# Two planes in turn for the last 40 experts of a mixture-of-experts sum, the third plane loaded early

## The chip, the core and the metric

The kernel runs on one core of a Trainium2 chip. The metric is the device time in microseconds of one execution, as the median of several runs.

## What is computed

Tokens `x` (4 x 1024 rows of 256 floats) go through a cross attention over 77 context rows and the tokens themselves, and then through a mixture of experts: each token picks 8 of 64 experts, every expert computes `silu(x Wg) * (x Wu)` times `Wd` for up to 256 tokens, and the results are weighted and added to the token's row. The part that matters here is the last:

```python
x = x + attention(...)
buf = zeros((E, CAP + 1, h)).at[e, pos_c].set(layernorm(x)[token])[:, :CAP]   # 64 experts, 256 slots each
g = einsum('ech,ehi->eci', buf, w_gate)
u = einsum('ech,ehi->eci', buf, w_up)
y = einsum('eci,eih->ech', silu(g) * u, w_down)
out = zeros((n, h)).at[token].add(y_slots * w_slot[:, None])
x = x + out
```

## The kernel before

The first 880 us are the attention and the routing, which scatters normalised rows, with token number and weights, into a table `slot_rows` in device memory: 256 slots for each of 64 experts. The change doesn't touch them.

The expert loop follows. For each expert e:
- SyncE (SP) loads its 256 slot rows into a ring of 8 buffers (`load_rows`, L975, 321 KB). From expert 8 on it waits until expert e-8 is weighed (`y_made`, L985). Behind the rows of experts 8 to 32, in the same loop, it loads the weights of experts 39 to 63 (L989, 384 KB); the first 39 experts' weights were loaded before.
- TensorE transposes the rows (L1305), multiplies with gate and up weights (L1321) and with the down weights (L1330); ScalarE copies and takes the silu (L1502, L1508), VectorE multiplies (`hidden`, L1743).
- VectorE weighs the result into one of 8 output buffers and takes the token numbers out (`weigh`, L1752, L1753). Expert e needs the buffer of e-8, so it waits until the addition of e-8 has landed (L1750).
- GpSimd (POOL) adds the 256 weighted rows to their tokens' rows in device memory: two indirect DMAs that accumulate, 128 rows of 1 KB each (L1111). Both wait for `y_made` and (L1110) for the plane.

A plane is a copy of the whole output in device memory (4096 rows and some dump rows). There are three: `out` (plane 0), which already holds the attention's result, and `sums` (planes 1 and 2), filled with zeros early on; the profile calls them `out_rows` and `sum`. Expert e is added to plane e % 3. Two experts often have the same token, and additions to one row must not overlap in time, so an expert waits until the one before it on its plane (e-3) has landed in full.

After the loop come the join and the store. SyncE waits for the last addition on plane 1 and loads it in four pieces of 1 MB (128 partitions x 8 KB), then the same for plane 2, then for plane 0 (L996). VectorE adds plane 2 to plane 1 (L1763) and the sum to plane 0 (L1766), piece by piece, and SyncE stores each piece (L1000). Every plane's pieces lie in on-chip memory that held weights or attention data before (`sum_at`, L801 on). Each engine runs its own instructions in the order in which they are written, and so does each queue of DMA issues.

Of the kernel before, what the change touches and what calls it, by code (L numbers as in the profile page):

```python
# [13 lines left out]
ALU = mybir.AluOpType  # L14
# [3 lines left out]
P = 128  # L18
# [13 lines left out]
E, TOPK, G, TG, CAP = 64, 8, 8, 4, 256  # L32
# [3 lines left out]
NTOK = B * S  # L36
# [7 lines left out]
RING = 8  # L44

PLANES = 3
JOIN_PARTS = 4


W_FREE = (16, 22, 39)  # L50
# [565 lines left out]
def build(nc, a, out):  # L616
    with ExitStack() as ctx:
        def sem(name):
            return ctx.enter_context(nc.semaphore(name))

        slot_rows = nc.dram_tensor("slot_rows", [E * CAP, ROW], F32).ap()

        sums = [nc.dram_tensor(f"sum{n}", [NTOK + DUMP, D], F32).ap() for n in range(1, PLANES)]
        names = ["x_loaded", "ctx_loaded", "wqkv_in", "wkvx_in", "qk_g_in", "misc_in", "mask_loaded", "mask_made", "ctx_masked",
                 "const_made", "empty_made", "pads_made", "filled", "vec_step", "pool_step", "stats_done", "z_made", "unit_full",
                 "emptied_act", "emptied_vec", "squares_summed", "rs_made", "normed", "hi_made", "lo_made", "ql_made",
                 "kb_copied0", "kb_copied1", "neg_made", "scores_full", "probs_made", "values_done",
                 "o_copied", "o_scaled", "xres_loaded", "xres_based", "x2_stored", "hn_scaled", "hn_made", "sel_made",
                 "slots_made", "rows_made", "scattered0", "scattered1",

                 *[f"w_early{n}" for n in range(3)], *[f"w_loaded{n}" for n in range(W_BUFS)],
                 *[f"x_in{n}" for n in range(RING)], "rows_turned", "turned_copied", "gate_up", "silu_made", "h_made",
                 "y_full", "y_made", *[f"added{n}" for n in range(PLANES)], *[f"sums{n}_in" for n in range(JOIN_PARTS)],
                 *[f"out{n}_in" for n in range(JOIN_PARTS)], "summed", "stored_out"]
        program(nc, a, out, slot_rows, sums, {n: sem(n) for n in names}, ctx)


# [50 lines left out]
def program(nc, a, out, slot_rows, sums, s, ctx):  # L688
    def sb(name, shape, dt=F32):
        return ctx.enter_context(nc.sbuf_tensor(name, shape, dt))  # L690
# [95 lines left out]
    def parts(t, count, size):  # L786
        return [t[:, size * n:size * (n + 1)] for n in range(count)]
# [11 lines left out]

    size = NTOK // P // JOIN_PARTS * D  # L800
    sum_at = [parts(K1_2, 2, size) + parts(Q0_2, 1, size) + parts(Q1a_2, 1, size),  # L801
              parts(pool_2, 3, size) + parts(Kb_2, 1, size), parts(K0_2, 2, size) + parts(Kb_2, 2, size)[1:]
              + parts(Q1b_2, 1, size)]
    row_ids = sb("row_ids", [P, RING, 2], U32)
    ps_x, ps_g, ps_y = (k.rearrange("p b (t q) -> p b t q", t=2) for k in (ps_s[:, 0:2], ps_u[:, 0:2], ps_o[:, 0:2]))
    slots_dram = slot_rows.rearrange("(e p t) r -> e p t r", p=P, t=2)
# [17 lines left out]
    for e in ("act", "dve"):  # L824
        n = 0
# [47 lines left out]
    def keys_of(pair):  # L873
        return slice(2 * PR, of_tiles(pair).stop)
# [10 lines left out]
    with ExitStack() as inner, nc.Block() as block:  # L885
# [3 lines left out]
        def _(sp):  # L889
# [84 lines left out]
            def load_rows(e):  # L974
                sp.dma_start(xr[e % RING], slots_dram[e]).then_inc(s[f"x_in{e % RING}"], 16)  # L975
# [4 lines left out]
            sp.wait_ge(s["x2_stored"], 16 * 2 * B)  # L980
            for e in range(RING):
                load_rows(e)
            for e in range(RING, E):

                sp.wait_ge(s["y_made"], e - RING + 1)  # L985
                load_rows(e)
                later = e - RING + W_BUFS
                if later < E:
                    sp.dma_start(w_at[later % W_BUFS], a["wexp"][later]).then_inc(s[f"w_loaded{later % W_BUFS}"], 16)  # L989

            plane_v = [k[0:NTOK, :].rearrange("(n p t) d -> n p (t d)", p=P, t=NTOK // P // JOIN_PARTS)
                       for k in (out, *sums)]
            for plane in (*range(1, PLANES), 0):
                sp.wait_ge(s[f"added{plane}"], 32 * len(range(plane, E, PLANES)))
                for n in range(JOIN_PARTS):
                    sp.dma_start(sum_at[plane][n], plane_v[plane][n]).then_inc(  # L996
                        s[f"sums{n}_in" if plane else f"out{n}_in"], 16)
            for n in range(JOIN_PARTS):
                sp.wait_ge(s["summed"], n + 1)
# [4 lines left out]
        def _(pool):  # L1004
# [44 lines left out]
            for t in plan.order["pool"]:  # L1049
# [14 lines left out]
                elif kind == "norm_q":  # L1064
                    b, pair = t[1:]
                    at = KEY_PAIRS * b + pair
                    mine = raw[:, at % 2, 0].rearrange("p a h d -> p a (h d)")
# [4 lines left out]
                elif kind == "lo":  # L1072
                    b, pair = t[1:]
                    at = KEY_PAIRS * b + pair
                    mine = keys_of(pair)
# [4 lines left out]
                elif kind == "ql":  # L1080
# [8 lines left out]
                    for i in range(2):  # L1089
                        mine = slice(PR * i, PR * (i + 1))  # L1090
# [14 lines left out]

            for e in range(E):
                pool.wait_ge(s["y_made"], e + 1)
                if e >= PLANES:
                    pool.wait_ge(s[f"added{e % PLANES}"], 32 * (e // PLANES))
                for t in range(2):  # L1110
                    pool.indirect_dma_start(  # L1111
                        out=(out, *sums)[e % PLANES],
                        out_offset=bass.IndirectOffsetOnAxis(ap=row_ids[:, e % RING, t:t + 1], axis=0),
                        in_=y_out[e % RING][:, t, :], in_offset=None, bounds_check=NTOK + DUMP - 1, oob_is_err=True,
                        compute_op=ALU.add).then_inc(s[f"added{e % PLANES}"], 16)

        @block.tensor
        def _(pe):
# [400 lines left out]
        def _(v):  # L1519
            n_vec = 0  # L1520

            def link(ins):
                nonlocal n_vec
                n_vec += 1
                ins.then_inc(s["vec_step"], 1)
                v.wait_ge(s["vec_step"], n_vec)
# [17 lines left out]
            for t in plan.order["dve"]:  # L1544
# [19 lines left out]
                elif kind == "rs":  # L1564
                    b, pair, piece = t[1:]
# [48 lines left out]
                elif kind == "scale":  # L1614
                    b, x, pr, half = t[1:]
                    mine = slice(2 * P * half, 2 * P * (half + 1))
# [18 lines left out]
                elif kind == "hn_scale":  # L1635
                    b, x, piece, q0, q1 = t[1:]
                    mine = slice(q0, q1)
# [107 lines left out]
            def weigh(e):  # L1745
                r = e % RING
                v.wait_ge(s["y_full"], e + 1)
                if e >= RING:

                    v.wait_ge(s[f"added{(e - RING) % PLANES}"], 32 * ((e - RING) // PLANES + 1))  # L1750
                for t in range(2):
                    v.tensor_scalar(y_out[r][:, t, :], ps_y[:, e % 2, t, :], xr[r][:, t, D + 1 + e:D + 2 + e], None, ALU.mult)  # L1752
                v.tensor_copy(row_ids[:, r, :].unsqueeze(2), xr[r][:, :, D:D + 1]).then_inc(s["y_made"], 1)  # L1753

            hidden(0)
            for e in range(1, E):
                hidden(e)
                weigh(e - 1)
            weigh(E - 1)
            for n in range(JOIN_PARTS):  # L1760
                v.wait_ge(s[f"sums{n}_in"], 16 * (PLANES - 1))
                for plane in range(2, PLANES):
                    link(v.tensor_tensor(sum_at[1][n], sum_at[1][n], sum_at[plane][n], ALU.add))  # L1763
            for n in range(JOIN_PARTS):
                v.wait_ge(s[f"out{n}_in"], 16)
                v.tensor_tensor(sum_at[0][n], sum_at[0][n], sum_at[1][n], ALU.add).then_inc(s["summed"], 1)  # L1766
# [44 lines left out]
```

## Time and profile before

| | us |
|---|---|
| median of 3 runs | 1169.75 (1168.24 to 1171.47) |
| span of the profiled execution (first to last instruction) | 1168.4 |
| TensorE busy | 906.8 (78%) |
| VectorE busy | 655.7 (56%) |
| GpSimd busy | 581.3 (50%) |
| ScalarE busy | 463.0 (40%) |
| expert loop, from GpSimd's first addition to its last issue | 889.1 to 1127.5 |
| join and store | 1127.5 to 1168.4 |

Busy shares of the span are averages over stages with different limits, so they don't tell what bounds the last 280 us. The rows below are of that stretch. Times in them are microseconds from the start of the span, unless a column says ns.

### The profile page before, as it was taken

The page shows a single profiled execution, that of the slowest core. Times are in us where ns is not written, and L with a number is a line of the kernel's source. Part 1 is how long each engine was busy: PE and PEld are TensorE (multiplying, and loading weights), DVE is VectorE, ACT ScalarE, POOL GpSimd, SP SyncE. Part 2 cuts the span into 40 slices and gives each one's busy share as a digit, 9 for nine tenths or more (in the row PEclk, how much of TensorE's full clock was granted, in tenths as well). Part 3 has the DMA queues.
Part 4 walks back from the last instruction along what each step waited for, and adds up shares of the span by engine and source line. Part 5 has one row for each costly group of instructions (what it writes and reads, how often), then busy time and mean ns, then how long its engine had stood idle before and what let it go on. Part 6 is the DMA issues. An engine that isn't in the chain of part 4 may idle for free.

```text
span 1168.4 us, 13234 instructions
## 1 busy us (share of the span) xinstructions
PE 906.8 (78%) x3848; PEld 626.7 (54%) x3848; DVE 655.7 (56%) x1956; ACT 463.0 (40%) x930; POOL 581.3 (50%) x522
## 2 busy tenths in 40 slices
PE   3869999999999999999964973957308999889300
PEld 2545666556656656656532542846207888777200
DVE  4475647875789775888652743743533443333206
ACT  3734675545755646664430521333103333222000
POOL 3530231204755635655665073155554888888850
PEclk9879999999999999999986995968658999999755
DMA  7739602012221422101261102000428999999689
GB/s 249 267 111 386 218 3 72 20 31 90 77 78 58 132 84 87 55 23 67 78 239 54 37 29 87 24 24 9 171 88 244 308 312 188 158 159 152 70 231 392
DMA packets 85335, 150.77 MB, mean 129 GB/s; under 512 B 14090, under 2 KB 53050, under 8 KB 83216
## 3 DMA queue, kind: packets, MB, share of 16 engines
q1 hardware_dynamic: 54543, 112.32, 27.8%
q0 software_dynamic: 30720, 37.61, 16.3%
q8 instruction: 32, 0.52, 0.2%
q14 instruction: 40, 0.32, 0.1%
HBM read 69.19 MB, written 97.45 MB: 143 GB/s over the span
## 4 chain that ended last, share of the span: by engine, by line
PE 48%; DVE 13%; issue 11%; POOL 8%; another core or an unknown queue 7%; DMA 7%; ACT 4%; POOLq 0%; SPq 0%; ACTq 0%; DVEq 0%
PE ps_o L1257 15%; PE ps_u L1154 6%; POOL sum L1111 4%; PE ps_s L1233 4%; PE ps_s L1235 4%; PE ps_u L1177 4%; DMA out_rows<-again,row_ids 3%; PE ps_u L1269 2%; PE ps_o L1252 2%; POOL out_rows L1111 2%; PE ps_u L1321 2%; DVE mp L1580 2%; PE ps_u L1165 2%; DMA sum<-again,row_ids 2%
## 5 line engine op out<-in xcount | busy, mean ns | idle before, releaser
L1044 POOL DMA_INDIRECT slot_rows<-rows,slot_idx x256 | 251.2, 981 | 312.0 <-issue 137.5
L1580 DVE TENSOR_REDUCE mp<-ps_u 128x1 f32<-128x512 f32 x256 | 165.1, 686 | 103.2 <-remote 49.6
L1450 ACT ACTIVATE probs<-ps_s 128x512 f32<-128x512 f32 x256 | 139.9, 596 | 176.6 <-PE ps_s L1235 105.4
L1111 POOL DMA_INDIRECT sum<-again,row_ids x84 | 130.0, 1548 | 26.5 <-issue 22.6
L1257 PE MATMUL ps_o<-probs,pool 128*128 128x512 f32 (+1 forms) x288 | 138.0, 602 | 2.5 <-ACT den L1471 2.5
L1321 PE MATMUL ps_u<-again 128*128 128x256 f32 x512 | 123.9, 386 | 0.0
L1257 PE MATMUL ps_o<-probs,V 128*128 128x512 f32 (+1 forms) x216 | 106.4, 615 | 10.4 <-ACT probs L1453 5.9
L1235 PE MATMUL ps_s<-qbT,Kb 65*128 65x512 f32 (+1 forms) x252 | 102.4, 406 | 0.0
L1752 DVE TENSOR_SCALAR again<-ps_o,again 128x256 f32<-128x256 f32 x128 | 56.1, 480 | 82.3 <-DMA sum<-again,row_ids 54.7
L1154 PE MATMUL ps_u<-wqkv_s,lnT 128*128 128x512 f32 (+1 forms) x256 | 97.4, 515 | 4.1 <-ACT lnT L1373 3.2
L1321 PEld LDWEIGHTS ps_u<-again 128*128 128x128 f32 x512 | 94.2, 194 | 11.0 <-issue 0.3
L1059 POOL TENSOR_TENSOR pool<-pool,rs_y 128x1024 f32<-128x1024 f32 (+1 forms) x20 | 33.0, 1649 | 131.9 <-DVEq L1575 130.8
L1111 POOL DMA_INDIRECT out_rows<-again,row_ids x44 | 68.3, 1551 | 27.4 <-DVE row_ids L1753 14.5
L1330 PE MATMUL ps_o<-again 128*128 128x256 f32 x256 | 67.1, 384 | 14.5 <-DVE again L1743 14.2
L1257 PEld LDWEIGHTS ps_o<-probs,pool 128*128 128x128 f32 (+1 forms) x288 | 53.4, 192 | 44.0 <-issue 28.1
L1502 ACT ACTIVATE again<-ps_s 128x512 f32<-128x512 f32 x64 | 38.2, 597 | 95.5 <-PE ps_s L1305 86.3
L1177 PE MATMUL ps_u<-K,Q 128*128 128x512 f32 x128 | 56.9, 518 | 22.6 <-DVE mp L1580 21.5
L1233 PE MATMUL ps_s<-Q,K 128*128 128x512 f32 x144 | 68.6, 476 | 4.5 <-issue 2.4
L1154 PEld LDWEIGHTS ps_u<-wqkv_s,lnT 128*128 128x128 f32 x256 | 48.9, 199 | 40.4 <-issue 27.8
L1743 DVE TENSOR_TENSOR again<-again,ps_u 128x256 f32<-128x256 f32 x64 | 26.8, 418 | 70.4 <-ACT again L1508 64.0
L1257 PEld LDWEIGHTS ps_o<-probs,V 128*128 128x128 f32 (+1 forms) x216 | 40.4, 195 | 43.0 <-issue 20.5
L1330 PEld LDWEIGHTS ps_o<-again 128*128 128x128 f32 x256 | 47.7, 190 | 25.7 <-DVE again L1743 19.7
(190 smaller groups left out, 1610.8 us busy)
## 6 DMA issues: line engine op xcount, KB each, us to landing
again<-in_wexp SPq DMA_DIRECT2D x64, 384.0 KB, 5.3
slot_rows<-rows SPq DMA_DIRECT2D x2, 10272.0 KB, 35.0
again<-slot_rows SPq DMA_DIRECT2D x64, 321.0 KB
sum<-rows SPq DMA_DIRECT2D x2, 4352.0 KB, 27.6
again<-sum SPq DMA_DIRECT2D x8, 1024.0 KB, 11.3
Kb<-K SPq DMA_DIRECT2D x16, 275.5 KB
pool<-in_x SPq DMA_DIRECT2D x4, 1024.0 KB, 5.5
xres<-in_x SPq DMA_DIRECT2D x8, 512.0 KB
```

The source lines that it names most:

```text
L1044: pool.indirect_dma_start(out=slot_rows, out_offset=bass.IndirectOffsetOnAxis(ap=slot_idx[x][:, q, k:k + 1], axis=0), in_=rows[x][:, q, :] ...
L1111: pool.indirect_dma_start(out=(out, *sums)[e % PLANES], out_offset=bass.IndirectOffsetOnAxis(ap=row_ids[:, e % RING, t:t + 1], axis=0), in ...
L1154: i = pe.matmul(dst, lnT[0:w, at % 2, c, 0:rj], rhs, start=(c == 0), stop=(c == 1))
L1177: pe.matmul(bank((*t, i))[:, :], queries(b, x)[0][:, 2 * pr + i, tile * P:(tile + 1) * P], K[b % 2][:, 2 * pr + i, half * 512:(half + 1) * ...
L1233: pe.matmul(dst, K[b % 2][:, h, kt * P:kt * P + rk], queries(b, x)[0][:, h, :], start=True, stop=False)
L1235: pe.matmul(dst, Kb[:, h, kt * P:kt * P + rk], qbT[block_no[(b, x, pr)] % 2][:, hh, :], start=False, stop=True).then_inc(s["scores_full"], 1)
L1257: i = pe.matmul(ps_o[:, hh, :], V[b % 2][0:rk, pr, kt, DH * hh:DH * hh + P], probs[0:rk, n % NPR, hh, :], start=(kt == 0), stop=(kt == NKT ...
L1321: i = pe.matmul(ps_g[:, e % 2, which, :], w_at[e % W_BUFS][:, o:o + I], xT[e % 2][:, k, :], start=(k == 0), stop=(k == 1))
L1330: i = pe.matmul(ps_y[:, e % 2, t, :], hid[e % 2][:, t * P:(t + 1) * P], w_at[e % W_BUFS][:, 4 * I:4 * I + D], start=True, stop=True)
L1450: act.activation(probs[:, n % NPR, hh, :], ps_s[:, u % NSC, :], ACT.Exp).then_inc(s["probs_made"], 1)
L1580: v.tensor_reduce(mp[:, i, tile, half:half + 1], bank((*t, i))[:, :], AX.X, ALU.max).then_inc(s["emptied_vec"], 1)
L1752: v.tensor_scalar(y_out[r][:, t, :], ps_y[:, e % 2, t, :], xr[r][:, t, D + 1 + e:D + 2 + e], None, ALU.mult)
```

## The change

Experts 0 to 23 are added to planes 0, 1, 2 in turn as before. Experts 24 to 63 are added to planes 1 and 0 in turn (24 to 1, 25 to 0, ... 62 to 1, 63 to 0). So every wait for a plane from expert 26 on is for the landing of e-2 instead of e-3, and plane 2 is complete when expert 23 has landed. Plane 2 is loaded in 16 pieces of 256 KB (128 partitions x 2 KB), one behind each of the row loads of experts 46 to 61, so when experts 38 to 53 have been weighed; ahead of the first stands a wait for plane 2's last addition. After the loop SyncE loads only plane 1 and plane 0. Some pieces of the planes get other places on chip. VectorE does the same eight additions as before.

```diff
+EARLY = 24
+EARLY_PIECES = 4
+EARLY_FROM = 46
+
+
+def plane_of(e):
+    return e % PLANES if e < EARLY else (e + 1) % (PLANES - 1)
+
+
+def plane_count(plane, end):
+    return sum(plane_of(e) == plane for e in range(end))
...
     sum_at = [parts(K1_2, 2, size) + parts(Q0_2, 1, size) + parts(Q1a_2, 1, size),
-              parts(pool_2, 3, size) + parts(Kb_2, 1, size), parts(K0_2, 2, size) + parts(Kb_2, 2, size)[1:]
-              + parts(Q1b_2, 1, size)]
+              parts(pool_2, 3, size) + parts(K0_2, 1, size),
+              parts(Kb_2, 2, size) + parts(probs_2, 1, size) + parts(Q1b_2, 1, size)]
...
                     sp.dma_start(w_at[later % W_BUFS], a["wexp"][later]).then_inc(s[f"w_loaded{later % W_BUFS}"], 16)
 
-            for plane in (*range(1, PLANES), 0):
-                sp.wait_ge(s[f"added{plane}"], 32 * len(range(plane, E, PLANES)))
+                piece = e - EARLY_FROM
+                if piece == 0:
+                    sp.wait_ge(s["added2"], 32 * plane_count(2, E))
+                if 0 <= piece < JOIN_PARTS * EARLY_PIECES:
+                    n = piece // EARLY_PIECES
+                    width = size // EARLY_PIECES
+                    mine = slice(width * (piece % EARLY_PIECES), width * (piece % EARLY_PIECES + 1))
+                    sp.dma_start(sum_at[2][n][:, mine], plane_v[2][n][:, mine]).then_inc(s[f"early{n}_in"], 16)
+
+            for plane in (1, 0):
+                sp.wait_ge(s[f"added{plane}"], 32 * plane_count(plane, E))
                 for n in range(JOIN_PARTS):
                     sp.dma_start(sum_at[plane][n], plane_v[plane][n]).then_inc(
                         s[f"sums{n}_in" if plane else f"out{n}_in"], 16)
...
                 pool.wait_ge(s["y_made"], e + 1)
-                if e >= PLANES:
-                    pool.wait_ge(s[f"added{e % PLANES}"], 32 * (e // PLANES))
+                plane = plane_of(e)
+                if plane_count(plane, e):
+                    pool.wait_ge(s[f"added{plane}"], 32 * plane_count(plane, e))
...
-                    v.wait_ge(s[f"added{(e - RING) % PLANES}"], 32 * ((e - RING) // PLANES + 1))
+                    plane = plane_of(e - RING)
+                    v.wait_ge(s[f"added{plane}"], 32 * plane_count(plane, e - RING + 1))
...
             for n in range(JOIN_PARTS):
-                v.wait_ge(s[f"sums{n}_in"], 16 * (PLANES - 1))
-                for plane in range(2, PLANES):
-                    link(v.tensor_tensor(sum_at[1][n], sum_at[1][n], sum_at[plane][n], ALU.add))
+                v.wait_ge(s[f"early{n}_in"], 16 * EARLY_PIECES)
+                v.wait_ge(s[f"sums{n}_in"], 16)
+                link(v.tensor_tensor(sum_at[1][n], sum_at[1][n], sum_at[2][n], ALU.add))
```

## Rows read from the trace of the kernel before

**Rows 1.** Timeline, GpSimd (start, duration, what, idle before): first addition, last five.

```profile
889.10 1.58 POOL L1111 DMA_INDIRECT out_rows<-again,row_ids  x1 [13.90 <-DVE row_ids L1753]
...
1118.51 1.54 POOL L1111 DMA_INDIRECT sum<-again,row_ids  x1 [0.30 <-issue]
1120.36 1.55 POOL L1111 DMA_INDIRECT sum<-again,row_ids  x1 [0.30 <-issue]
1122.22 1.54 POOL L1111 DMA_INDIRECT sum<-again,row_ids  x1 [0.30 <-issue]
1124.07 1.55 POOL L1111 DMA_INDIRECT out_rows<-again,row_ids  x1 [0.30 <-issue]
1125.92 1.54 POOL L1111 DMA_INDIRECT out_rows<-again,row_ids  x1 [0.30 <-issue]
```

**Rows 2.** The page's costliest groups: busy us, mean ns of one, idle before.

```profile
L1111 POOL DMA_INDIRECT sum<-again,row_ids x84 | 130.0, 1548 | 26.5 <-issue 22.6
```

**Rows 3.** Waits from 880 to 1130 us: us in total, times, longest.

```profile
DVE again L1752 <- DMA sum<-again,row_ids: 54.7, 24, 5.3
...
POOL sum L1111 <- DMA sum<-again,row_ids: 1.5, 2, 0.9
POOL sum L1111 <- DMA out_rows<-again,row_ids: 1.2, 4, 0.3
```

**Rows 4.** Windows: length, busy PE, PEld, DVE, ACT, POOL; clock, DMA share, GB/s.

```profile
926.00:963.00 37.00, 37.00 (x197) 32.56 (x197) 17.24 (x49) 11.97 (x25) 29.82 (x21) 1.00 1.10 308
1002.00:1064.00 62.00, 52.12 (x258) 43.58 (x258) 21.85 (x69) 15.70 (x32) 51.94 (x34) 0.97 0.92 159
...
1138.00:1158.00 20.00, 0.00 (x0) 0.00 (x0) 16.01 (x7) 0.00 (x0) 0.00 (x0) 0.50 1.01 427
```

**Rows 5.** Timeline, VectorE: weighing that starts as experts 22, 28, 32, 42, 48, 55 land.

```profile
980.41 0.88 DVE L1752 TENSOR_SCALAR again<-ps_o,again 128x256 f32<-128x256 f32 x2 [2.27 <-DMA sum<-again,row_ids]
...
1002.99 0.88 DVE L1752 TENSOR_SCALAR again<-ps_o,again 128x256 f32<-128x256 f32 x2 [5.33 <-DMA sum<-again,row_ids]
...
1016.85 0.88 DVE L1752 TENSOR_SCALAR again<-ps_o,again 128x256 f32<-128x256 f32 x2 [4.41 <-DMA sum<-again,row_ids]
...
1054.78 0.88 DVE L1752 TENSOR_SCALAR again<-ps_o,again 128x256 f32<-128x256 f32 x2 [5.33 <-DMA out_rows<-again,row_ids]
...
1075.56 0.88 DVE L1752 TENSOR_SCALAR again<-ps_o,again 128x256 f32<-128x256 f32 x2 [3.81 <-DMA out_rows<-again,row_ids]
...
1100.10 0.88 DVE L1752 TENSOR_SCALAR again<-ps_o,again 128x256 f32<-128x256 f32 x2 [2.78 <-DMA sum<-again,row_ids]
```

**Rows 6.** Timeline, GpSimd: the second addition of expert 22.

```profile
973.89 1.56 POOL L1111 DMA_INDIRECT sum<-again,row_ids  x1 [0.30 <-issue]
```

**Rows 7.** Chain that ended last (start, us, what): two landings, weights being loaded.

```profile
928.34 7.12 DMA sum<-again,row_ids
...
939.47 7.15 DMA sum<-again,row_ids
```

**Rows 8.** From a release to GpSimd's start: chain at expert 18, timeline before expert 0.

```profile
955.78 0.04 issue
955.82 0.03 POOLq L1111
...
956.58 1.55 POOL out_rows L1111
...
888.09 0.16 DVE L1753 CAST row_ids<-again 128x2 uint32<-128x2 f32 x1
```

**Rows 9.** One line, L975: the row loads' issues (ns min/median/max, first, last start).

```profile
L975 SPq DMA_DIRECT2D again<-slot_rows x64: 319/320/710, 876.4 to 1071.5; - x64
```

**Rows 10.** The join: timeline of SyncE and VectorE, and two pieces of the chain.

```profile
1122.32 11.73 SPq L996 DMA_DIRECT2D again<-sum  x8
1138.60 1.76 SPq L996 DMA_DIRECT2D again<-out_rows  x4
...
1125.92 12.66 DMA out_rows<-again,row_ids
...
1139.93 18.27 DMA again<-out_rows
...
1158.22 2.29 DVE L1766 TENSOR_TENSOR again<-again 128x2048 f32<-128x2048 f32 x1 [0.18 <-DMA again<-out_rows]
```

More of the change, by code:

```diff
@@ L633, in build @@
                  "y_full", "y_made", *[f"added{n}" for n in range(PLANES)], *[f"sums{n}_in" for n in range(JOIN_PARTS)],
-                 *[f"out{n}_in" for n in range(JOIN_PARTS)], "summed", "stored_out"]
+                 *[f"early{n}_in" for n in range(JOIN_PARTS)], *[f"out{n}_in" for n in range(JOIN_PARTS)], "summed", "stored_out"]
         program(nc, a, out, slot_rows, sums, {n: sem(n) for n in names}, ctx)
@@ L982, in _ @@
                 load_rows(e)
+            plane_v = [k[0:NTOK, :].rearrange("(n p t) d -> n p (t d)", p=P, t=NTOK // P // JOIN_PARTS)
+                       for k in (out, *sums)]
             for e in range(RING, E):
@@ L989, in _ @@
                     sp.dma_start(w_at[later % W_BUFS], a["wexp"][later]).then_inc(s[f"w_loaded{later % W_BUFS}"], 16)
-            plane_v = [k[0:NTOK, :].rearrange("(n p t) d -> n p (t d)", p=P, t=NTOK // P // JOIN_PARTS)
-                       for k in (out, *sums)]
-            for plane in (*range(1, PLANES), 0):
-                sp.wait_ge(s[f"added{plane}"], 32 * len(range(plane, E, PLANES)))
+                piece = e - EARLY_FROM
[8 more added lines that the diff above has]
+                sp.wait_ge(s[f"added{plane}"], 32 * plane_count(plane, E))
                 for n in range(JOIN_PARTS):
@@ L1107, in _ @@
                 pool.wait_ge(s["y_made"], e + 1)
-                if e >= PLANES:
-                    pool.wait_ge(s[f"added{e % PLANES}"], 32 * (e // PLANES))
+                plane = plane_of(e)
+                if plane_count(plane, e):
+                    pool.wait_ge(s[f"added{plane}"], 32 * plane_count(plane, e))
                 for t in range(2):
                     pool.indirect_dma_start(
-                        out=(out, *sums)[e % PLANES],
+                        out=(out, *sums)[plane],
                         out_offset=bass.IndirectOffsetOnAxis(ap=row_ids[:, e % RING, t:t + 1], axis=0),
                         in_=y_out[e % RING][:, t, :], in_offset=None, bounds_check=NTOK + DUMP - 1, oob_is_err=True,
-                        compute_op=ALU.add).then_inc(s[f"added{e % PLANES}"], 16)
+                        compute_op=ALU.add).then_inc(s[f"added{plane}"], 16)
         @block.tensor
```

## The prediction

> **What bounds the kernel now.** I read the profile from its end backwards, because the change touches the last 280 us only. The first view is the timeline of GpSimd (POOL). It issues two accumulating DMAs for each of the 64 experts, from 889.10 to 1125.92 us [rows 1]. A DMA costs 1.55 us of GpSimd time [rows 2] and 0.30 us pass before the next, so an expert costs 3.71 us (1120.36 to 1124.07) [rows 1]. 64 experts at 3.71 us are 237 us, and the stretch from 889.10 to 1127.47 is 238.4 us: GpSimd issues back to back for the whole loop. The list of waits says the same from the other side. VectorE waits 54.7 us for additions to land, because its ring of eight outputs is full, while GpSimd's waits for a landing are of 0.3 to 0.9 us each [rows 3]. TensorE, ScalarE, VectorE and the loads are ahead of GpSimd, and only GpSimd's issue, then the join of the planes after 1127.47 us, sets the end. The chain that ended last names VectorE and DMAs in places in this stretch; these are coincidences in time, since GpSimd had no idle time there.
>
> The join is bound by the DMA engines: from 1138 to 1158 us their share is 1.01 at 427 GB/s [rows 4]. One plane is 4.19 MB, thus 4.19 / 0.427 = 9.8 us.
>
> **What a landing takes, and who waits for it.** This decides the case. An expert may be added to a plane only when the previous expert on that plane has landed. I call L the time from the end of an expert's second issue to its landing. The profile gives no landing directly for every expert, but VectorE starts to weigh expert e+8 0.1 us after e has landed, so its rows give L [rows 5]. The ends of the issues follow from one row, 973.89 + 1.56 = 975.45 us for expert 22 [rows 6], and 3.707 us for each expert after it.
> - Quiet, after the last row load (expert 55): landing at 1100.0, issue ended at 1097.8, L = 2.2 us.
> - With the slots' rows being loaded (321 KB for each expert), L alternates. The short ones are 2.2 to 3.2 us. The long ones, on even experts from 22 to 48, are 4.9, 3.9, 4.2, 5.2, 3.2, 4.2, 4.7, 3.8, 4.2, 4.2, 5.1, 3.6, 3.1 and 3.6 us; the rows of 22, 28, 32, 42 and 48 stand in the group [rows 5].
> - With weights loaded too (705 KB for each expert, 308 GB/s in all instead of 159 [rows 4]), the chain shows 7.12 and 7.15 us from the start of a second issue, so L = 5.6 us [rows 7].
>
> How late may a landing be? After a landing GpSimd needs time to start. At 955.82 us its sequencer takes up expert 18, whose plane had just been freed, and the DMA starts at 956.58; with the 0.04 us ahead of that it is 0.80 us [rows 8]. The very first DMA agrees: VectorE's row ends at 888.25, the DMA starts at 889.10, 0.85 us [rows 1, 8]. I take 0.84. With three planes the wait is for expert e-3, two whole experts (7.41 + 0.30 us) lie between, and L may be 6.9 us. The case of expert 18 is the only one in which a landing exceeded that, and so the wait is as good as free now. With two planes only one expert lies between: 3.71 + 0.30 - 0.84 = 3.16 us. **Every landing over 3.16 us stalls GpSimd by the difference**, and GpSimd is the bound.
>
> **Part 1, two planes from expert 24 on.** The wait at line 1110 becomes one for e-2. Behind it on GpSimd's queue stands only the next expert, but VectorE, SyncE's row loads and TensorE hang on the same landings, and all of them have slack. Putting the 14 long landings as they were against 3.16 us gives 1.7 + 0.7 + 1.0 + 2.0 + 0 + 1.0 + 1.6 + 0.6 + 1.0 + 1.1 + 1.9 + 0.4 + 0 + 0.4 = 13.4 us. The odd experts use the other plane, and their landings stay under 3.2 us, so they add nothing. After expert 48 L is 2.2 us, and nothing stalls. Of these, experts 22 to 28 have 5.4 us and 30 to 46 have 7.6 us. Does a stall heal itself by letting the loads pass first? Partly it may. But a landing also releases the row load (SyncE's issue follows it through VectorE), and in the stalled order expert e+2's second DMA goes out 0.84 + 3.40 = 4.2 us after e's landing, when these loads are on their way. So I do not count on it.
>
> **Part 2, sixteen loads of 256 KB during experts 38 to 53.** Line 985 lets them go when those experts are weighed, so at the landings of experts 30 to 45, at about 1008 to 1064 us. Their issue costs SyncE about 0.3 us each, as the row loads do [rows 9], which is hidden since SyncE waits for VectorE most of that time. The second issue of expert 23 ends at 979.2 us (one step behind that of 22 [rows 6]); with any landing seen here it is down by 987, and the first piece comes after 1008 us, so the added wait for plane 2 does not hold the row loads queued behind it. What they cost is landing time. Bytes per expert rise from 321 to 577 KB; the nearest rows on either side are the long landings here (4.0 us on average for 30 to 46) and those under weights at 705 KB (5.6 us). At the unchanged pace the line between them gives 4.0 + 256/384 x 1.6 = 5.1 us; a stalled loop, with about 4.5 us to an expert, moves 577/4.5 = 128 GB/s of loads against 321/3.71 = 87 before and 705/3.71 = 190 under weights, and by that measure it is 4.0 + 41/103 x 1.6 = 4.6 us. I take 4.6, since the pace will be the stalled one. Two experts then share one stall of 4.6 - 3.16 = 1.44 us: 8.5 x 1.44 = 12.2 us for experts 30 to 46 instead of 7.6. Bounds: the loads add nothing and part of the 13.4 us heals, which I put at 8 us, or L reaches the 5.6 us seen with weights (8.5 x 2.44 = 20.7, in all 26.5 us).
>
> Loop, taken value: 5.4 + 12.2 + 0.4 = **18.0 us longer**, between 8 and 26.5.
>
> **Part 3, the join.** Now: loads of plane 1 issued at 1122.32, when expert 61 has landed, 5.15 us ahead of GpSimd's end T = 1127.47; the last addition starts at 1158.22 = T + 30.75; the span ends at 1168.4, 10.2 us later [rows 10]. After: 4.19 MB less, 9.8 us off. Against it plane 1 now ends with expert 62, so its loads begin one expert later relative to T, 3.7 us. In its favour the stream meets fewer additions: today those of experts 62 and 63 land inside it (the last one 12.66 us after its issue began [rows 10]), four DMAs; afterwards at most those of 63. Each reads 128 KB here and 128 KB of the plane; 0.26 MB at 427 GB/s are 0.6 us, so about 2 us for three of them. Sum: 9.8 - 3.7 + 2.1 = **8.2 us shorter**. Bounds are 6 (no relief, a short gap before the loads of the last plane) and 9.8. VectorE has the same eight additions, all but the last behind loads. New places of the buffers and the extra semaphores cost nothing on a path.
>
> Sum: 1168.4 + 18.0 - 8.2 = 1178.2 us of span. The median of the runs stands 1.35 us above this span, so **1179.5 us** is forecast.
>
> A rule of the Trainium skill is weighed here, in sentences that nothing else needs. In the trace a quiet landing takes L = 2.2 us [rows 5, 6]. The page "DMA: Bandwidth & Descriptors", section "Anatomy of one DMA", gives a GpSimd DMA a fixed 2.0 us plus its bytes over 436 GB/s, so an estimate of 2.3 us for 128 KB, and calls the fixed part about constant. By that rule alone no landing would reach 3.16 us and part 1 would be free; the quiet rows agree, the rows under load (3.2 to 5.6 us) don't, and the measurement decides. The same page says (section "SWDGE vs HWDGE vs iDMA") that an engine serves its queues in turn, which speaks against the change: every load's packets would stand between an addition's. In the join, with megabytes of loads on the way, the last addition lands 12.66 - 1.55 = 11.1 us after its issue [rows 10], which agrees.
>
> **The rivals.**
> - *Faster: landings stay short.* The stalls shift the additions so far that the loads pass between them and L stays at the quiet 2.2 us or little above. For it: every second landing in the stretch already is under 3.2 us. Against it: 12 of the 14 others are over, and the new loads hang on the same landings. It decides where all stalls together are under 8.2 us. Only the join's gain is left, 1169.75 - 8.2 = 1161.5 us, up to 1166 with a few stalls.
> - *Even: the loop loses what the join gains.* The stalls are 5 to 12 us: the loads add nothing and part of the 13.4 us heals. That is 1166.5 to 1173.5 us, about 1169.
> - *Slower still: contention as with weights.* L = 5.6 us while the pieces run: 1169.75 + 26.5 - 8.2 = 1188 us. For it: the DMA share already is 0.92 there [rows 4]. Against it: fewer bytes than with weights.
> - *The early load saves nothing in the join* since the last addition's landing, not the loads, sets it. With the last landing at T + 11.1 as now and 4.19 MB behind it the join would still be some 7 us shorter; this changes the sum by 1 to 2 us and lies inside the range.
>
> **How the numbers follow.** My forecast's mechanism with 12 to 23 us of stall (1173.5 to 1184.5): 0.62. Even: 0.16. Faster: 0.10. Slower still, over 23 us: 0.12. The range is 1167 to 1190 us: it leaves out the faster rival and the far ends. A measurement of this kernel can tell 0.3%, 3.5 us, from no change. Faster by more: 0.10; within: 0.16; slower by more: 0.74.
>
> **What would show it.** In the profile after: GpSimd's last issue ends at about 1145 instead of 1127.5, with idle times of 0.5 to 2 us ahead of every second expert from 24 to 48, released by DMAs on out_rows and sum (wrong if they stay at 0.30); none after expert 50. From GpSimd's end to the end of the span 32 to 34 us instead of 40.9. The DMA share from 1010 to 1075 at about 1.0 and over 190 GB/s. The early loads land well before the join. The prediction is wrong if landings under the early loads stay below 3.2 us, or if SyncE or VectorE, not a landing, becomes what GpSimd waits for.

## The result

The changed kernel takes 1181.96 us, the kernel before 1168.99 us (medians of 6 runs each on one chip). The ratio is 1.0107 (95% interval 1.0083 to 1.0131): the change makes the kernel 13 us slower. The profiled execution has a span of 1179.4 us against 1168.4. These 11.0 us split into three parts that the trace gives directly:

| us | before | after | difference |
|---|---|---|---|
| start of the first addition | 889.1 | 891.5 | +2.4 |
| loop, first addition to the end of the last issue | 238.4 | 254.5 | +16.1 |
| join, from there to the end of the span | 40.9 | 33.4 | -7.5 |

The first part lies ahead of everything that was changed. The same start is anywhere from 886.8 to 892.2 in the profiles of five other kernels below with unchanged work ahead of it, so it is not counted as an effect.

### The profile page after: what moved, and what is told of

The parts are those of the page before. It is cut to its first block, busy times and chain, and to the rows that moved or that the text cites. A ratio compares the mean times of both kernels' runs of the same rounds, so it can differ in the third digit from the quotient of the medians.

```text
span 1179.4 us, 13247 instructions
## 1 busy us (share of the span) xinstructions
PE 914.5 (78%) x3848; PEld 631.8 (54%) x3848; DVE 654.0 (55%) x1956; ACT 462.5 (39%) x930; POOL 580.4 (49%) x522
## 4 chain that ended last, share of the span: by engine, by line
PE 52%; DVE 12%; issue 11%; POOL 8%; DMA 6%; another core or an unknown queue 5%; ACT 5%; POOLq 0%; SPq 0%; ACTq 0%; DVEq 0%
PE ps_o L1278 16%; PE ps_u L1175 6%; PE ps_s L1254 4%; PE ps_u L1198 4%; PE ps_s L1256 4%; POOL sum L1132 4%; PE ps_u L1342 3%; POOL out_rows L1132 3%; DMA out_rows<-again,row_ids 3%; PE ps_o L1273 2%; PE ps_u L1290 2%; PE ps_u L1186 2%; DMA sum<-again,row_ids 2%; PE ps_o L1351 2%
## 5 line engine op out<-in xcount | busy, mean ns | idle before, releaser
L1132 POOL DMA_INDIRECT sum<-again,row_ids x72 | 111.4, 1548 | 29.7 <-issue 18.4
L1132 POOL DMA_INDIRECT out_rows<-again,row_ids x56 | 86.7, 1549 | 40.6 <-issue 16.9
L1351 PE MATMUL ps_o<-again 128*128 128x256 f32 x256 | 71.3, 403 | 24.5 <-DVE again L1764 24.4
```

What stands on the lines that cost most here:

```text
L1132: pool.indirect_dma_start(out=(out, *sums)[plane], out_offset=bass.IndirectOffsetOnAxis(ap=row_ids[:, e % RING, t:t + 1], axis=0), in_=y_o ...
L1351: i = pe.matmul(ps_y[:, e % 2, t, :], hid[e % 2][:, t * P:(t + 1) * P], w_at[e % W_BUFS][:, 4 * I:4 * I + D], start=True, stop=True)
```

## The profile after

First GpSimd's timeline around experts 35 to 40 (start, duration, what, idle before and what ended it). Before, every idle time here was 0.30 us. Two rows belong to each expert; 1026.29 is the first of expert 35.

```profile
1026.29 1.55 POOL L1132 DMA_INDIRECT out_rows<-again,row_ids  x1 [1.57 <-DMA out_rows<-again,row_ids]
1028.14 1.55 POOL L1132 DMA_INDIRECT out_rows<-again,row_ids  x1 [0.30 <-issue]
1029.99 1.55 POOL L1132 DMA_INDIRECT sum<-again,row_ids  x1 [0.30 <-issue]
1031.84 1.54 POOL L1132 DMA_INDIRECT sum<-again,row_ids  x1 [0.30 <-issue]
1035.19 1.55 POOL L1132 DMA_INDIRECT out_rows<-again,row_ids  x1 [1.80 <-DMA out_rows<-again,row_ids]
1037.04 1.56 POOL L1132 DMA_INDIRECT out_rows<-again,row_ids  x1 [0.30 <-DVE row_ids L1775]
1038.91 1.56 POOL L1132 DMA_INDIRECT sum<-again,row_ids  x1 [0.31 <-issue]
1043.34 1.54 POOL L1132 DMA_INDIRECT sum<-again,row_ids  x1 [2.87 <-DMA out_rows<-again,row_ids]
1045.19 1.55 POOL L1132 DMA_INDIRECT out_rows<-again,row_ids  x1 [0.30 <-issue]
1047.04 1.54 POOL L1132 DMA_INDIRECT out_rows<-again,row_ids  x1 [0.31 <-issue]
1049.36 1.55 POOL L1132 DMA_INDIRECT sum<-again,row_ids  x1 [0.77 <-DMA sum<-again,row_ids]
```

VectorE's timeline shows two of the landings (it starts 0.1 us after one), those of experts 35 and 37:

```profile
1034.44 0.88 DVE L1774 TENSOR_SCALAR again<-ps_o,again 128x256 f32<-128x256 f32 x2 [5.55 <-DMA out_rows<-again,row_ids]
...
1042.98 0.88 DVE L1774 TENSOR_SCALAR again<-ps_o,again 128x256 f32<-128x256 f32 x2 [5.72 <-DMA out_rows<-again,row_ids]
```

L is again the time from the end of an expert's second issue to its landing. Expert 35's second issue ends at 1029.69 and it lands at 1034.35, so L = 4.7 us. Expert 37, next on its plane, starts 0.84 us later, at 1035.19, and GpSimd has idled 1.80 us instead of 0.30. That is the stall as the prediction has it, 4.7 - 3.16 = 1.5 us. The other kind was not foreseen. At 1043.34 the **second** DMA of expert 38 (on plane 1) starts 2.6 us late, though expert 38 waits for nothing between its two DMAs. It starts 0.46 us after the landing of expert 37 at 1042.88, the one for which the **next** expert, 39, waits.

Adding up these rows over the loop (each idle time less the usual 0.30): 10.2 us at first DMAs, nearly all of it at nine between experts 29 and 52, and 7.5 us at second DMAs: experts 38 (2.6) and 45 (3.1), and 7, 19, 31 and 59 with 0.4 to 0.5 each. Before, the two kinds were 0.4 and 0.9 us.

The list of waits of GpSimd from 963 to 1150 us (us in total, times, longest) tells the same with the usual 0.30 in it, against [rows 3]:

```profile
POOL out_rows L1132 <- issue: 13.2, 33, 3.4
POOL sum L1132 <- issue: 12.3, 40, 0.4
POOL out_rows L1132 <- DMA out_rows<-again,row_ids: 7.3, 5, 1.9
POOL sum L1132 <- DMA sum<-again,row_ids: 6.2, 5, 1.9
POOL sum L1132 <- DMA out_rows<-again,row_ids: 2.9, 1, 2.9
POOL out_rows L1132 <- DMA sum<-again,row_ids: 1.9, 3, 0.8
```

Windows as in [rows 4] (length, busy PE, PEld, DVE, ACT, POOL; clock, DMA share, GB/s). GpSimd is busy 44.43 of 62 us instead of 51.94; more is moved (185 GB/s instead of 159), and yet the DMA share fell from 0.92 to 0.86. Fewer additions in the same time fit this: in no_rows_no_pieces (below), where only additions are under way, they alone take a DMA share of 0.61 for 70 GB/s (920 to 980 us).

```profile
1002.00:1064.00 62.00, 51.16 (x235) 42.26 (x236) 17.69 (x56) 14.14 (x29) 44.43 (x30) 0.92 0.86 185
```

The join, which answers to [rows 10], in the timeline. Plane 1's loads are issued at the landing of expert 62, plane 0's at that of 63, and the last addition of the planes starts at 1169.23, 23.3 us after GpSimd's end at 1145.95 (30.75 before).

```profile
1144.47 2.04 SPq L1016 DMA_DIRECT2D again<-sum  x4
...
1154.55 1.76 SPq L1016 DMA_DIRECT2D again<-out_rows  x4
...
1169.23 2.29 DVE L1788 TENSOR_TENSOR again<-again 128x2048 f32<-128x2048 f32 x1 [0.18 <-DMA again<-out_rows]
```

## The experiments

The time of a run scatters by several us, and one chip ran all kernels some 85 us faster than the others (before: 1086 us on it, about 1170 elsewhere; the clock granted to TensorE was 0.92 there against 0.89). On it ran no_rows_pieces, no_rows_no_pieces, ring2048 and the first switch_51. The loop and the join are read from the trace of each kernel; switch_51, profiled on the fast chip and on a slower one, has 241.5 us of loop on both, so they are compared across chips. The loop is the stretch from the first addition to the end of the last issue, as above. "First" and "second" are the idle times at first and second DMAs, less 0.30 each. Most rows are a single profile.

| | loop | first | second | join |
|---|---|---|---|---|
| before | 238.4 | 0.4 | 0.9 | 40.9 |
| after | 254.5 | 10.2 | 7.5 | 33.4 |
| planes_only | 247.2 | 5.3 | 5.1 | 43.5 |
| loads_only | 237.5 | 0.0 | 0.5 | 40.6 |
| no_rows_pieces | 246.9 | 2.8 | 7.3 | 34.1 |
| no_rows_no_pieces | 240.0 | 0.0 | 3.0 | 42.9 |
| spaced_waits | 257.7 | 12.6 | 8.3 | 33.2 |
| ring2048 | 269.6 | 4.8 | 27.9 | 33.1 |
| ring5120 | 250.9 | 13.6 | 0.6 | 33.6 |
| late_switch | 245.1 | 4.3 | 3.7 | 34.7 |
| switch_51 (two profiles) | 241.5, 241.5 | 2.4, 2.4 | 2.2, 2.1 | 33.4, 33.9 |

**planes_only: two planes, no early load.** Plane 2 is loaded in the join behind plane 1.

```diff
-                piece = e - EARLY_FROM
...
-            for plane in (1, 0):
+            for plane in (1, 2, 0):
```

> The changed kernel, but plane 2 is loaded in the join, behind plane 1, in 4 pieces of 1 MB; no early loads. Theory (a landing over 3.16 us stalls GpSimd by the difference, and the early loads lengthen the landings): the loop is 8 to 13 us longer than before (254.5 us in the changed kernel, 238.4 before), so 3 to 8 us less than in the changed kernel; the join is 3.7 us less the saved additions, so 1 to 3 us longer than the 40.9 us of before. In all 10 to 16 us over before. Rival (the early loads are what costs, the planes are free): the loop stays within 2 us of 238.4 and the time within 1 to 4 us of before. Rival (the early loads cost nothing): the loop is 254 us as in the changed kernel, and the time 17 to 20 us over before.

Loop 247.2, join 43.5 us. Timed, it is 1.0161 of before (1.0118 to 1.0204), 1188.0 against 1172.4 us; the trace explains 8.8 + 2.6 = 11.4 of these 15.6 us, the rest is open. Neither rival holds: the two planes alone cost 8.8 us of the loop, the early loads the other 7.3. And the early load brings 43.5 - 33.4 = 10.1 us in the join, near the 9.8 us reckoned for one plane. So the early load by itself gains 10.1 - 7.3 = 2.8 us; what loses are the two planes that make room for it, 8.8 us in the loop and 2.6 in the join. GpSimd's waits from 963 to 1136 us:

```profile
POOL sum L1123 <- DMA out_rows<-again,row_ids: 3.2, 4, 1.8
POOL sum L1123 <- DMA sum<-again,row_ids: 2.9, 3, 1.4
POOL out_rows L1123 <- DMA sum<-again,row_ids: 2.7, 3, 1.6
POOL out_rows L1123 <- DMA out_rows<-again,row_ids: 2.2, 2, 1.3
```

**loads_only: three planes, with extra loads.** They read the input x, so nothing of the sums is left out.

```diff
-    return e % PLANES if e < EARLY else (e + 1) % (PLANES - 1)
+    return e % PLANES
...
-                    sp.dma_start(sum_at[2][n][:, mine], plane_v[2][n][:, mine]).then_inc(s[f"early{n}_in"], 16)
+                    sp.dma_start(sum_at[2][n][:, mine], x_v[n][:, mine]).then_inc(s[f"early{n}_in"], 16)
```

> Three planes throughout as before, but with 16 extra loads of 256 KB at the places of the early loads; they read the input x instead of a plane (same shape) and are overwritten in the join, where all three planes are loaded as before. Theory: the long landings of experts 30 to 45 rise from 4.0 to 4.3 or more us on average, but with three planes they may take 6.9 us, so GpSimd issues back to back, the loop stays 238 to 239 us and the time is within 0.3% of before. Rival (the loads slow GpSimd's own work or the DMA engines are at their limit): gaps or longer issues on GpSimd, loop over 241 us.

Ratio 0.9985 (0.9955 to 1.0015), loop 237.5. The loads do what they were expected to do to the landings: of each two experts from 30 to 46 the later landing takes 4.6 us on average, 4.1 without the loads, and the mean of all rises from 3.3 to 4.1. With three planes GpSimd doesn't wait for it. Here the loads have no price of their own; they have one through a wait that is short of slack. GpSimd's waits, none over 0.3 us, and the windows row from 1010 to 1070, with a DMA share of 1.04:

```profile
POOL sum L1133 <- DMA out_rows<-again,row_ids: 0.3, 1, 0.3
...
1010.00:1070.00 60.00, 50.90 (x255) 41.36 (x255) 20.97 (x66) 15.70 (x32) 50.25 (x33) 1.00 1.04 224
```

**no_rows_pieces and no_rows_no_pieces: the row loads taken away.** The changed kernel and planes_only, both with

```diff
+                if e < LAST_ROWS:
                     load_rows(e)
```

where `LAST_ROWS` is 40; TensorE's wait for the rows is changed to match.

> The changed kernel without the row loads of experts 40 to 63: these experts work on the rows left in the ring (loads left out, so the output is not the reference's). The early loads stay. So from the landing of expert 24 on only 256 KB follow each landing instead of 577 KB. Theory (the landing is lengthened by what is loaded at the same time): long landings fall to 3 to 4 us, stalls and late second DMAs together to 2 to 7 us instead of 17.7 in the changed kernel, loop 240 to 245 us. Rival (an addition lands late for a reason of its own, the plane's rows or a shorter distance between additions to one plane): landings of 4 us and more and a loop over 250 us.

> As the kernel with two planes and the whole plane 2 loaded in the join (planes_only), but also without the row loads of experts 40 to 63 (they work on the rows left in the ring, so the output is not the reference's). Nothing is loaded between the landing of expert 24 and the join. Theory: every landing from 26 on takes 2.2 to 2.4 us, under 3.16, so there is no stall and no late second DMA on two planes, and the loop is 238 to 240 us as with three planes; the join stays 43 to 44 us. Rival (two planes stall by themselves): stalls at every second expert as in planes_only, loop 245 us or more.

With nothing loaded, every landing from expert 25 to 55 takes 2.1 to 2.4 us (VectorE's rows show no later ones), and no first DMA waits. So the distance of one expert is enough by itself, and the stalls at first DMAs come from what is loaded beside. One expectation failed: second DMAs are late here too, by 0.5 to 0.6 us at experts 31, 38, 45, 52 and 59, always 0.46 us after the landing of the expert before. VectorE's rows show three landings 3.7 us apart, as GpSimd issues, the quiet case:

```profile
908.03 0.88 DVE L1767 TENSOR_SCALAR again<-ps_o,again 128x256 f32<-128x256 f32 x2 [2.08 <-DMA out_rows<-again,row_ids]
...
911.74 0.88 DVE L1767 TENSOR_SCALAR again<-ps_o,again 128x256 f32<-128x256 f32 x2 [2.43 <-DMA sum<-again,row_ids]
...
915.50 0.88 DVE L1767 TENSOR_SCALAR again<-ps_o,again 128x256 f32<-128x256 f32 x2 [2.49 <-DMA out_rows<-again,row_ids]
```

With the early loads only, the first DMAs' stalls are 2.8 us, but both kinds together are 10.1 us against the expected 2 to 7, and the loop is 246.9, over the expected 245, again through the second DMAs of 38 and 45 (2.4 and 2.0 us). Landings of 4.1 and 4.2 us are still seen (experts 33, 37, 40), over the expected 3 to 4. The rival, an addition that is late for a reason of its own, is refused by no_rows_no_pieces, not by this kernel.

**spaced_waits and ring2048: what makes second DMAs late?** The late ones on two planes are at most of 31, 38, 45, 52 and 59, 14 DMAs apart. (Among the first experts, on three planes, they are at some of 7, 13 and 19, 12 apart.) Two edits, one in the instruction stream and one in the size of the memory in which GpSimd writes its descriptors:

```diff
+                for _ in range(2):
+                    pool.wait_ge(s["filled"], 16 * FILLS)
```

```diff
-    nc = bacc.Bacc("TRN2", target_bir_lowering=False, num_devices=1, dynamic_dma_scratch_size=4096)
+    nc = bacc.Bacc("TRN2", target_bir_lowering=False, num_devices=1, dynamic_dma_scratch_size=2048)
```

> The changed kernel with two more instructions on GpSimd behind each expert's second DMA, waits on a semaphore that has long been full. In the changed kernel the second DMAs of experts 38 and 45 start 2.6 and 3.1 us late, both 0.46 us after the landing for which the next expert waits, as if the wait behind the DMA held it. If that is so and depends on where the wait lies in the instruction stream, the late second DMAs vanish or are at other experts than 31, 38, 45 and 59, and the time is up to 6 us less. If they are due to the data or to the loads, they stay at 38 and 45 and the time is that of the changed kernel.

> The changed kernel with half the on-chip memory for the descriptors that GpSimd writes (2048 bytes instead of 4096, the compiler's setting). So far the second DMAs that start late are 14 DMAs apart at most places (experts 31, 38, 45, 52, 59), whatever stands in the instruction stream. If they belong to the wrap of this memory, they come twice as often: every 7 DMAs, so every 3 or 4 experts, at second DMAs and perhaps at first ones, and the loop is 5 to 12 us longer than 254.5. If they don't, they stay at 38 and 45 and the loop at 253 to 258 us.

The additional waits left them where they were (38 by 3.2 us, 45 by 3.4), ratio 1.0118 (1.006 to 1.0175). But they left only one row of their own in the trace in place of 128, so it is open whether they changed what GpSimd executes, and as a test of the instruction stream this is weak. The halved memory is clear: late second DMAs at 27, 30, 33, 36, and so on to 63, every 3 experts, 27.9 us in all (2.5 of it at six of the first 20 experts), and the loop is 269.6 us. The expected loss was 5 to 12 us, the measured one 15.1. Three of them in GpSimd's timeline, each ended by the other plane's landing:

```profile
930.84 1.55 POOL L1132 DMA_INDIRECT sum<-again,row_ids  x1 [2.72 <-DMA out_rows<-again,row_ids]
...
945.67 1.56 POOL L1132 DMA_INDIRECT out_rows<-again,row_ids  x1 [4.01 <-DMA sum<-again,row_ids]
...
961.11 1.54 POOL L1132 DMA_INDIRECT sum<-again,row_ids  x1 [4.09 <-DMA out_rows<-again,row_ids]
```

**ring5120: as much of that memory as fits** (the same edit, with 5120).

> The changed kernel with 5120 instead of 4096 bytes for GpSimd's descriptors, all that still fits beside the buffers. With 2048 bytes the late second DMAs came every 3 experts instead of every 7. If they go with the size, they come now every 8 or 9 experts (17 or 18 DMAs), not at both 38 and 45, and together cost 2 to 6 us instead of 7.5; loop 250 to 254 us. If only a power of two counts, they stay at 7 experts.

The late second DMAs of 38 and 45 are gone, 0.6 us of that kind is left in all, less than the expected 2 to 6, and the loop is 250.9. The first DMAs' stalls are 13.6 us, more than the 10.2: it seems that part of what the late DMAs had taken is paid there. But the first addition starts at 905.0 us, against 887 to 892 in the kernels with 4096 bytes on such a chip, so the stage before lost 13 us or more (one run, 1191.2 us). Why is open.

**late_switch: the switch at expert 48.** The three planes go on to expert 47; the 16 pieces of plane 2 follow in a loop of their own:

```diff
+            for piece in range(JOIN_PARTS * EARLY_PIECES):
+                e = EARLY_FROM + piece
+                sp.wait_ge(s[f"added{plane_of(e)}"], 32 * plane_count(plane_of(e), e + 1))
```

> The same change moved to where landings are short: experts 0 to 47 on three planes, 48 to 63 on two, and the 16 pieces of plane 2 are issued one at each landing of experts 47 to 62, after the last row load. Theory: a landing is 2.2 us there, and one piece of 256 KB at a time lifts it to no more than about 3, so the loop costs 0 to 4 us more than 238.4; the join is 33 to 34 us instead of 40.9 us, and the time is 3 to 8 us under before. Rival (a piece lengthens a landing as the rows do, to over 4 us): stalls of 1 us at every second expert, 8 us in all, and the time is that of before.

Ratio 0.9994 (0.9964 to 1.0024), no gain. The loop costs 6.7 us, over the expected 4; the join gains 6.2. The first experts on two planes, 48 and 50, stalled by 1.5 and 1.6 us, because experts 46 and 48 still met row loads (L 4.7 and 4.4); two second DMAs (55, 62) were late by 3.2 us together.

**switch_51: the switch at expert 51**, the loads in 12 pieces at the landings of experts 50 to 61, in a loop of their own as in late_switch.

```diff
-EARLY = 24
-EARLY_PIECES = 4
-EARLY_FROM = 46
+EARLY = 51
+EARLY_PIECES = 3
+EARLY_FROM = 50
```

> Experts 0 to 50 on three planes, 51 to 63 on two, the third plane loaded in 12 pieces of 344 or 336 KB at the landings of experts 50 to 61. With the switch at 48 the loop was 6.7 us longer than before, of it 3.1 us at experts 48 and 50, whose landings (4.7 and 4.4 us) still met row loads. Theory: these 3.1 us go, the rest (1.2 us of stalls, 3.2 us at two late second DMAs) stays within 2 to 6 us because the pieces are a third larger; loop 241 to 244.5 us, join 34 to 35 us, time 1 to 4 us under before, which may not be clear of the noise. Rival (the larger pieces lift landings over 4 us): loop 246 us or more, time as before or above.

> The kernel with the switch at expert 51 once more, in the same call as the one with 5120 bytes. Before the loop 238.4 us and join 40.9 us; there 241.5 and 33.4: 3 to 5 us under before if the join's gain holds, the time of before if the first result was chance.

> The kernel with the switch at expert 51 and 5120 bytes for the descriptors. There one late second DMA of 1.65 us was left among the experts on two planes; with fewer such places 0 to 1.7 us less, loop 239.5 to 241.5 us, time 3 to 6 us under before. Rival: the place falls on an expert with a longer landing, and nothing is gained on the kernel with 4096 bytes.

Ratio 0.9971 (0.9953 to 0.9988), and 0.9961 (0.9941 to 0.998) the second time, on another chip: 3 to 5 us faster than the kernel before, and the best of all. Loop 241.5 both times, join 33.4 and 33.9 us, as expected. Landings there are not as short as in the quiet, 2.8 to 3.9 us for experts 51 to 55, but they pass the 3.16 us by little, and no first DMA is over 0.6 us late. With 5120 bytes the loop is 240.2, as expected, but the time is not: the first addition starts at 900.2 against 891.1 us, and the ratio is 1.0019 (1.0001 to 1.0038). Of these 9.1 us 6.3 are there already in the routing, where GpSimd's addition to `xres` starts at 782.6 instead of 776.3 us. GpSimd's additions to plane 0 in the profile of the first (ns min/median/max, first and last start) and its waits from 875 to 1045 us:

```profile
L1130 POOL DMA_INDIRECT out_rows<-again,row_ids x48: 1544/1548/1583, 802.4 to 1042.4; - x48
...
POOL sum L1130 <- DMA out_rows<-again,row_ids: 2.9, 4, 2.0
POOL out_rows L1130 <- DMA out_rows<-again,row_ids: 1.8, 2, 0.9
```

## Why the prediction was right

It gave 1179.5 us, slower at a chance of 0.74; measured are 1181.96. The direction and the cause are right; that the total is so near is luck in part, because two errors cancelled. Stalls at first DMAs, the step that was argued, are 10.2 us (9.8 more than before) and not 18.0, which is what the even rival had said (5 to 12 us); a second kind of stall that nobody had foreseen made up most of the difference. ring5120, where that kind is all but gone, shows what the argued step gives alone: 12.5 us more loop, just inside the forecast's 12 to 23, and in a single profile.

- *GpSimd bounds the loop, and a landing over 3.16 us stalls it by the difference.* Right. With L = 4.7 us for expert 27 its successor 29 stalled 1.6 us, with 4.4 for 33 expert 35 stalled 1.3, and no_rows_no_pieces has neither long landings nor stalls at first DMAs.
- *Part 1, 13.4 us from the landings as they were.* The term was too large. planes_only stalls 5.3 us at first DMAs. The later landing of each two from 30 to 46 is 3.4 us there, not 4.1 as before. That the stalled loop spaces its loads would explain it, and I had said not to count on that; no run tests it by itself. Together with the late second DMAs the loop grew by 8.8 us.
- *Part 2, L of 4.6 us under the early loads, 4.6 us more loop.* L was 4.4 us for the later of two in the changed kernel, near the forecast. The price was 254.5 - 247.2 = 7.3 us. Of it 4.9 us are at first DMAs (10.2 against 5.3), near the forecast, and 2.4 at second ones (7.5 against 5.1), because L also sets how late those of 38 and 45 are.
- *Loop 18.0 us longer.* 16.1 measured, but only 9.8 by the step that was argued. The other 6.6 us (7.5 less 0.9; the two add up to 16.4, within the reading of the rows) are the second DMAs, a step that the prediction lacked. The trace of before showed one: in it expert 19's second DMA starts 0.64 us late, 0.46 us after the landing for which expert 20 waits. It is the longest wait of 0.9 us in [rows 3], which the prediction passed over. Take these 6.6 us away and not all of them would be gained: ring5120's loop is only 3.6 us shorter.
- *Join 8.2 us shorter.* 7.5 measured. The early load gives 10.1 us, against 9.8; the later start of plane 1's loads costs 2.6 us net (planes_only), where 3.7 - 2.1 = 1.6 had been reckoned. (The relief of 2.1 us is three times 0.6 by the prediction's own working, so 1.8; no row gives 2.1.) The rival that the early load saves nothing is refuted.
- *The idle rows that would show it.* Right for the first DMAs at every second expert, but they changed from odd to even experts behind the late DMA of 38 and back behind that of 45, and expert 52 still waits 0.7 us, where none was expected after 50. From 1010 to 1075 us the core moves 191 GB/s as forecast, but at a DMA share of 0.87, not about 1.0.
- *The faster rival, landings that stay short.* Refuted for the changed kernel. The Trainium skill's figure of an about constant 2.0 us (page "DMA: Bandwidth & Descriptors", section "Anatomy of one DMA") agrees with the quiet case alone, 2.1 to 2.4 us in no_rows_no_pieces, if it is counted from the end of GpSimd's instruction. switch_51 comes out ahead because its two-plane stretch lies where landings are shorter.

Of the 13.0 us between the medians the loop and the join explain 8.6. Another 2.4 us in the profiled runs came before the loop, and the remaining 2.0 us are not placed: they are within the scatter of the runs. planes_only has a surplus of 4.2 us that I can't place either.

## What to carry to other kernels

When buffers are taken away from a rotation, compare the time until a buffer is free with the time that its reuse leaves, transfer by transfer and under the load that will be there, not the mean and not the quiet value: here 3.16 us were left, and 2.2 or 4.7 us were needed depending on what else was loading. Ask of each half of such a change what it is worth by itself: here the early load gained 2.8 us and the smaller rotation lost 11.4. A transfer that is hidden can still lengthen the ones beside it, and that is paid where a wait has little slack. So it paid here to move both, the smaller rotation and the extra loads, into the stretch where nothing else is loaded: a trade of 16 us in the loop for 7.5 us in the join became one of 3 us for 7 us when the switch went from expert 24 to 51 and the loads behind it, in 12 pieces instead of 16.

## What was not expected of the hardware

- At regular places GpSimd starts an indirect DMA only 0.46 us after the wait of the instructions **behind** it is met. On two planes, with 4096 bytes for its descriptors, that is at every seventh expert (14 DMAs), with 2048 at every third (6 DMAs), with 5120 at neither 38 nor 45. The idle time at such DMAs was 7.5 us in the changed kernel and 27.9 us with 2048 bytes; the loop was 3.6 us shorter with 5120 bytes and 15.1 us longer with 2048. That it goes with this memory is shown, the mechanism is not.
- Giving the descriptors 5120 bytes instead of 4096 went with a start of the expert loop 9 us later on the same chip (900.2 against 891.1), in a stage in which nothing else was changed. It was seen in both kernels with 5120 bytes and is unexplained.
- Accumulating DMAs of 128 KB land 2.2 us after the end of their issue in quiet. Beside 321 to 577 KB of loads for each expert the later landing of each two takes 3 to 5 us, and beside 705 KB two landings took 5.6 us, although the transfers' own bytes didn't change.
- With nothing else under way these additions alone took 0.61 of the DMA engines' time while 70 GB/s were moved; megabyte loads of planes took 1.01 for 427 GB/s ([rows 4]).
